# A graph network kernel: six quads of columns made by TensorE in the first layer in place of five, and 40 columns of a chunk gathered in place of 44

## What is computed

```python
W_rel = jnp.matmul(w_comp, V).reshape(num_rels, in_dim, out_dim)     # 90 matrices
e = jnp.concatenate([z_src, z_e, z_dst], axis=1) @ Wa.T              # a score of the edge
msg = jnp.einsum('ei,eio->eo', h_src, W_rel[rel_type]) * e           # first layer
h_out = jax.ops.segment_sum(msg, dst, num_segments=n_nodes)
...
A = edge_emb[edge_type].reshape(-1, MSG_DIM, HID_DIM)                # 8 matrices
msg = jnp.einsum('emh,eh->em', A, h_src)                             # second layer
m = jax.ops.segment_sum(msg, edge_dst, num_segments=N_NODES)         # then a GRU cell
```

## Time and profile before

| | us |
|---|---|
| median of 3 runs | 10946.74 |
| lowest and highest | 10932.45, 10950.66 |
| the profiled execution | 10932.0 |
| its span, first to last instruction | 10930.1 |

### The profile page before, as it was taken

The page is one execution under the profiler, slowest core; times in us unless marked ns, Lnnn a source line. Parts: engine busy times, 40 slices in busy tenths (PEclk is TensorE's granted clock), DMA queues, the critical chain, the costliest instruction groups (busy, mean ns, idle before and its releaser), DMA issues.

```text
span 10930.1 us, 139324 instructions
## 1 busy us (share of the span) xinstructions
PE 5779.2 (53%) x53821; PEld 4786.9 (44%) x53821; DVE 4059.6 (37%) x8932; ACT 4413.2 (40%) x5373; POOL 4678.1 (43%) x4885
## 2 busy tenths in 40 slices
PE   2455555555555555555455555555555555555554
PEld 0244444444444444444344445444544544454453
DVE  2353333344444333333433333333333333333333
ACT  2444334344444433434334344334433443443343
POOL 5434444444444444444344433343344334433434
PEclk6677777777777777777667777777777777776775
DMA  5400000010000001000101101101110111011011
GB/s 157 175 17 21 22 22 22 20 22 22 22 22 22 18 22 22 22 20 22 34 20 10 10 8 10 10 8 10 10 10 8 10 10 10 9 10 10 8 10 12
DMA packets 650830, 252.54 MB, mean 23 GB/s; under 512 B 533184, under 2 KB 623673, under 8 KB 649654
## 3 DMA queue, kind: packets, MB, share of 16 engines
q10 hardware_dynamic: 421870, 84.39, 4.5%
q0 software_dynamic: 156128, 44.51, 4.2%
q1 hardware_dynamic: 72296, 115.06, 3.0%
HBM read 78.24 MB, written 164.99 MB: 22 GB/s over the span
## 4 chain that ended last, share of the span: by engine, by line
PE 48%; issue 42%; ACT 4%; another core or an unknown queue 4%; DMA 1%; DVE 1%; ACTq 0%; SPq 0%; POOL 0%; DVEq 0%; POOLq 0%
PE ps_table L688 39%; PE ps_table L698 5%; PE ps_misc L664 3%; ACT hot_key L872 2%; DMA relation_table<-scanned 1%; ACT hot_type L873 0%; ACT scanned L844 0%; PE ps_table L808 0%; ACTq L828 0%; PE ps_misc L763 0%; DVE scanned L1155 0%; PE ps_table L776 0%; ACT hot_key L877 0%; PE ps_hist L763 0%
## 5 line engine op out<-in xcount | busy, mean ns | idle before, releaser
L688 PE MATMUL ps_table<-node_parts,hot_key 128*128 128x192 bf16 (+1 forms) x44928 | 4668.7, 260 | 2775.8 <-issue 2770.1
L688 PEld LDWEIGHTS ps_table<-node_parts,hot_key 128*128 128x128 bf16 x44928 | 4005.6, 102 | 3362.3 <-issue 3284.4
L872 ACT ACTIVATE hot_key<-ps_misc,less_key 128x512 bf16<-128x512 f16 x3744 | 2216.7, 703 | 5980.5 <-remote 4455.5
L516 POOL DMA_INDIRECT rows<-type_table,idx x2184 | 2065.5, 946 | 3093.1 <-DVE scanned L1155 2418.3
L516 POOL DMA_INDIRECT rows<-relation_table,idx x2288 | 2229.8, 975 | 2674.8 <-DVE scanned L1155 1982.2
L1191 DVE TENSOR_TENSOR picked<-ps_table,hot_tile 128x416 f32<-128x416 f32 x936 | 542.3, 579 | 5272.2 <-remote 4725.4
L877 ACT ACTIVATE hot_key<-hot_key,ones 128x3072 bf16<-128x3072 bf16 (+1 forms) x468 | 1513.9, 3235 | 15.3
L664 PE MATMUL ps_misc<-ident_f,match_cols 128*128 128x128 f16 x3848 | 410.4, 230 | 999.1 <-issue 952.1
L1196 DVE TENSOR_REDUCE source<-picked 128x32 f32<-128x416 f32 x936 | 806.6, 862 | 32.1
L664 PEld LDWEIGHTS ps_misc<-ident_f,match_cols 128*128 128x128 f16 x3848 | 277.1, 101 | 1111.8 <-issue 1045.8
L1205 DVE TENSOR_REDUCE rows<-by_in 128x32 f32<-128x512 f32 (+1 forms) x988 | 694.2, 703 | 33.8
(11 more groups left out here) (207 smaller groups left out, 2037.1 us busy)
## 6 DMA issues: line engine op xcount, KB each, us to landing
scanned<-scanned ACTq DMA_DIRECT2D x52, 992.0 KB
relation_table<-scanned SPq DMA_DIRECT2D x50, 765.0 KB
relation_table<-t_buf SPq DMA_DIRECT2D x48, 765.0 KB
rows<-relation_table,idx POOLq DMA_INDIRECT x2288
rows<-type_table,idx POOLq DMA_INDIRECT x2184
scanned<-scanned ACTq DMA_DIRECT2D x52, 496.0 KB, 7.6
he<-in_edge_attr SPq DMA_DIRECT2D x52, 434.0 KB
type_table<-t_buf SPq DMA_DIRECT2D x14, 448.0 KB
```

Source lines behind the costliest of these rows:

```text
L516: pool.indirect_dma_start(out=rows[:, k, :], out_offset=None, in_=table, in_offset=bass.IndirectOffsetOnAxis(ap=index[:, k:k + 1], axis=0) ...
L688: pe.matmul(ps_table[duo][:, 0, t * BLOCK_W:t * BLOCK_W + width], hot_key[:, b, g, edges], node_parts[:, part, g:TILES:BLOCKS, :], start=( ...
L872: act.activation(hot_key[:, b, g, :], match_bank[:, 0, :], ACT.Abs, bias=less_key[:, g:g + 1])
```

## The change

The number of quads becomes a pair, six for the first layer and five for the second. So the first layer makes 2 + 5 x 4 = 22 columns and gathers 40. The buffers that hold keys and picks of a chunk's made columns grow from 20 to 22 columns. The 32 scans of the chunk before, which were shared out as 0, 4, 8, 12 and 8 over five steps, are shared out as 0, 4, 6, 8, 8 and 6 over six. Scan 15 was the fourth of the fourth step's scans and is now the sixth of the fourth step's. All other edits replace the constant by the layer's own number.

```diff
-QUADS = 5
+QUADS = (6, 5)
...
+        self.quads = QUADS[n]
...
-        self.widths = [DUO] * known + [QUAD] * (QUADS - known)
+        self.widths = [DUO] * known + [QUAD] * (self.quads - known)
         self.share = sum(self.widths)
         self.own = CHUNK - self.share
...
     def half(self, parity, q):
 
-        return (parity * (QUADS - self.known) + q - self.known) % 2
+        return (parity * (self.quads - self.known) + q - self.known) % 2
...
+    SHARE = max(quads * QUAD - known * (QUAD - DUO) for quads, known in zip(QUADS, KNOWN))
...
-        hot_tile = sb("hot_tile", [P, 2, QUADS * QUAD, BLOCK_TILES])
+        hot_tile = sb("hot_tile", [P, 2, SHARE, BLOCK_TILES])
...
             def chunk_by_products(lay, m, parity, last):
 
-                for q in range(QUADS):
-                    if lay.known <= q < QUADS - 1:
+                for q in range(lay.quads):
+                    if lay.known <= q < lay.quads - 1:
                         spread_quad(lay, m, parity, q + 1)
-                    if q == QUADS - 1 and not last:
+                    if q == lay.quads - 1 and not last:
                         spread_quad(lay, m + 1, 1 - parity, lay.known)
                     for duo in range(lay.widths[q] // DUO):
-                        if lay.known and (q, duo) == (QUADS - 2, 1) and not last:
+                        if lay.known and (q, duo) == (lay.quads - 2, 1) and not last:
                             spread_quad(lay, m + 1, 1 - parity, 0)
                         products(lay, m, parity, q, duo)
...
-            SCAN_WITH = (range(0), range(4), range(4, 12), range(12, 24), range(24, 2 * D))
+            SCAN_WITH = (range(0), range(4), range(4, 10), range(10, 18), range(18, 26), range(26, 2 * D))
```

More of the change, by code:

```diff
@@ L659, in spread_quad @@
                 pe.wait_ge(keys_set[lay.n], m + 1)
-                wait_past(pe, match_sb[lay.n], m * QUADS + q)
+                wait_past(pe, match_sb[lay.n], m * lay.quads + q)
                 for k in range(int(q < lay.known), 2):
@@ L668, in products @@
             def products(lay, m, parity, q, duo):
-                quad = m * QUADS + q
+                quad = m * lay.quads + q
                 pe.wait_ge(match_set[lay.n], quad + 1)
@@ L679, in products @@
                 if q >= lay.known:
-                    before = (m, q - 1) if q > lay.known else (m - 1, QUADS - 1)
+                    before = (m, q - 1) if q > lay.known else (m - 1, lay.quads - 1)
                     wait_past(pe, products_used[lay.n], lay.done(*before, duo))
@@ L693, in products @@
                     hot = hot_known[:, :]
-                before = (m, q - 1) if q > 0 and duo * DUO < lay.widths[q - 1] else (m - 1, QUADS - 1)
+                before = (m, q - 1) if q > 0 and duo * DUO < lay.widths[q - 1] else (m - 1, lay.quads - 1)
                 wait_past(pe, products_used[lay.n], lay.done(*before, duo))
@@ L865, in one_hot @@
                 else:
-                    before = (m, q - 2) if q - 2 >= lay.known else (m - 1, q - 2 + QUADS - lay.known)
+                    before = (m, q - 2) if q - 2 >= lay.known else (m - 1, q - 2 + lay.quads - lay.known)
                     wait_past(act, products_ps[lay.n], lay.done(*before, 1))
@@ L884, in chunks_out @@
                 ahead = lay.known + 1
-                for q in range(1 - lay.known, QUADS):
+                for q in range(1 - lay.known, lay.quads):
                     one_hot(lay, 0, 0, q)
@@ L893, in pair @@
                         if not (last and h == 1):
-                            for q in range(ahead, QUADS):
+                            for q in range(ahead, lay.quads):
                                 one_hot(lay, m, 1 - h, q)
@@ L1217, in chunk_rows @@
             def chunk_rows(lay, m, parity, last, between=lambda q: None):
-                steps = m * ((QUADS - lay.known) * ROW_STEPS + 1) + 1
-                for q in range(QUADS):
+                steps = m * ((lay.quads - lay.known) * ROW_STEPS + 1) + 1
+                for q in range(lay.quads):
                     base = steps + (q - lay.known) * ROW_STEPS
-                    if q == QUADS - 3 and not last:
+                    if q == lay.quads - 3 and not last:
                         keys(lay, m + 1, 1 - parity, base)
-                    if q >= QUADS - 3 and not last:
+                    if q >= lay.quads - 3 and not last:
                         base = base + 1
-                    if q + 1 < QUADS or not last:
-                        rest_one_hot(lay, m * QUADS + (q + 1), lay.half(parity, q + 1))
+                    if q + 1 < lay.quads or not last:
+                        rest_one_hot(lay, m * lay.quads + (q + 1), lay.half(parity, q + 1))
                     make_rows(lay, m, parity, q, base, between)
@@ L1284, in pair @@
                     if last and h == 1:
-                        for q in range(QUADS):
+                        for q in range(layers[0].quads):
                             with_quad(q)
@@ L1487, in pair @@
                     if last and h == 1:
-                        for q in range(QUADS):
+                        for q in range(layers[1].quads):
                             with_quad(q)
```

8 lines of the change are left out of this document (4 added, 4 removed).

## The result

| | before | after |
|---|---|---|
| median, us | 10948.7 | 11352.41 |
| lowest and highest | 10932.45, 10951.68 | 11346.32, 11362.29 |
| span of the profiled execution | 10930.1 | 11347.2 |

The changed kernel is slower by 404 us, ratio 1.0373 (95% interval 1.0355 to 1.0391). The forecast was 11290 us, within 11190 to 11430.

A forecast was written before the change was run, and what follows sets the result against it. Gathering and TensorE's work were taken to add. 50 chunks x (9.92 - 5.6 + 0.7) = 251, plus 84 for turns, plus 9, gave +344 us, so 11276, and 11290 us by the runs' median; range 11190 to 11430.

The forecast's parts named there:

- engines independent: Rival: the stop has another cause and 40 gathers end it no sooner; +635 us, 11580 us; chance 3%.
- the stop: Stretch of slowed TensorE during a chunk's gathers, 62.6 us for 44 in the first layer, about 1.4 us per gather.
- The added quad: First layer: one more full quad costs 9.92 us a chunk, as none of it can hide in the stop.
- four gathers: First layer: four gathers fewer shorten the stop by 4 x 1.4 = 5.6 us a chunk.
- The stop's edge: Stop may begin sooner (up to 3.6 us a chunk, +130 us); first gather may shorten (-48 us); neither was taken.
- The loop's turn: First layer: PE's turn after the last quad leaves the stop; 3.5 us for each of 24 turns, 84 us.
- the turn stays hidden: Rival: the first-layer loop's turn still costs nothing; 11206 us, chance 10%.
- What lies in the stop: First layer: the known pair leaves the stop and cheap matmuls take its place; +0.7 us a chunk, from 0 to 0.9.
- The quad in the stop: Rival: the added quad's matmuls fit into the stop, so the kernel gets faster; 10656 us, chance 4%.
- PE starves in it: Rival: ACT cannot make the known pair's one-hot in the stop, PE waits; +95 us, 11385 us; chance 20%.
- The early stop: Stop beginning 5.7 us after the first gather, not 9.3; up to 3.6 us a chunk; 11420 us with starving PE.
- The signs named beforehand: First layer: gathers every 99 us, 102 to 104 every second; full pace after 56 to 57 us; second layer unchanged.

The follow-up runs named there:

- e11: Changed kernel with gathers released one step later and TensorE's first-layer loop written out four times: 11211.09 us, ratio 1.0266 to the kernel before.
- e12: Kernel before with four quads in both layers (48 and 46 gathers), run where the stop exists: 10559.01 us, ratio 0.9507.
- e6: Kernel before, unedited, run in a place without the stop: 6339.41 us.
- e5: Changed kernel, unedited, run in a place without the stop: 6190.98 us, ratio 0.9758 to the kernel before.
- e4: Kernel before with four quads in both layers (48 and 46 gathers), run without the stop: 6901.2 us, ratio 1.0875.

## Why the prediction was right

**The bound.** For the place of its trace the reading holds: gathering and PE's work add. Seven burst lengths lie on one line, 40 gathers for 56.2 us, 42 for 59.0, 44 for 62.6, 46 for 64.8, 48 for 67.6, 84 for 117.8 and 96 for 135.5 (1.40 to 1.42 each). Opposite changes of the number of quads moved the time in opposite directions, +3.7% and -4.9%. But "engines independent", the rival to which I gave 3%, is how the same kernel behaves in another place: there PE passes its duos at full pace amid the gathers and all follows from POOL's beat. The prediction rested on a property of the place and had no row that could tell it from one of the kernel. That the first result came from a place with the stop was luck, for the sign too: of the seven places of this case three have it, and in one of the other four this very change won 2.4%. The Trainium skill's page "Trainium Architecture — The Big Picture", section "Inside one NeuronCore", says that the engines run in parallel and synchronize only through semaphores. For TensorE beside POOL's gathers that agrees with the runs at 6346 us and not with those at 10949 us.

**The added quad, 9.92 us, and four gathers, -5.6.** Right in sum: +4.75 a chunk in e11 against +4.3. There is no run with one of the two alone under the stop.

**The stop's edge, two unknowns left at nothing.** Both occurred. The first gather fell from 1.91 to 0.94 us, and full pace came back after 56.2 us where e11 with its slow first gather has 57.0: -0.8. The stop began 6.9 us after the first gather in place of 8.4: +1.5 to +1.7. My bounds were +3.6 and -0.96. In sum +0.7 to +0.9 a chunk: the period without a turn grew by 100.1 - 94.2 = 5.9 us where I had 5.0, 46 us over 50 chunks. This is the larger of the two terms that were mis-sized; I took neither unknown, as if they cancelled, though one bound was nearly four times the other.

**The loop's turn, 3.5 us.** The chunks with it are 4.4 us longer than those without. Such pairs differ by 0.6 us before and 0.9 in e11 in any case, so the turn itself is worth 3.6 to 3.9. The gap itself is 2.6 us, the low end of what I read in the second layer. The rest goes with the clock: the nine chunks whose clock stays up behind the gap take 102.9 us, 2.7 over those without a turn, which is the gap alone; the 14 in which it drops take 105.6, 2.8 more. At 2213.93 the six matmuls take 1.54 us and the way to the second next transposes 12.2 us (to 2226.15), where from 2419.46 they take 0.87 and 10.7. The second layer's two gaps of the earlier trace rows were the right rows to take it from. That the turn stays hidden (10%) is refuted by the row at 2213.93, and e11 shows what would have kept it hidden.

**What lies in the stop, +0.7.** The known pair's six matmuls are outside of it (2213.93, 1.54 us at a lower clock or 0.87), as predicted. The 0.7 itself does not follow from my rows: 0.86 - 6 x 0.09 is 0.3. And the stop passed 34 or 35 matmuls, not 40 "whatever they are". The pair's cost can't be told from that of the edge; together they are 5.9 - 4.3 = 1.6 us.

**The sum.** 344 us by forecast, 417 between the spans: 73 too few. Two chunks were to grow by 2 x 5.02 + 3.5 = 13.5 us and grew by 204.7 - 188.4 = 16.3; 25 pairs make 70 us. 46 are the edge of the stop, as above. The other 0.9 us a pair, 23 us, lie in the chunks with the turn: I had 3.5 us for it, and gap and clock make 4.4 (2.7, and 2.8 in 14 of 23). I had left out that the clock can drop behind the gap.

**The other rivals.** The quad in the stop: 30 to 38 matmuls pass in it, fewer than before, so no. PE starves in it, because ACT can't make the known pair's one-hot: ACT makes it within the stop, at 2162.73.

```profile
2162.73 0.47 ACT L875 ACTIVATE hot_known<-ps_misc,less_type 90x256 bf16<-90x256 f16 x1 [11.61 <-remote]
```

The early stop that went with that rival did come, at less than half its upper price of 3.6 us; my 11420 us for the two together allowed only 35 us for it, against the 130 of the paragraph before. The signs named beforehand were right in full pace (56.2), in the beat of 99 and 102 to 104 (100 and 105), in one gap of 2.6 us in every second chunk and in the second layer. The waits of ACT over 1 us at full pace, named as a sign against me, are there: 6.51 us behind the turn, and 1.2 to 2.9 us in the chunks without one, in which PE has no gap.

```profile
2318.14 4.73 ACT L874 ACTIVATE hot_key<-ps_misc,less_key 128x512 bf16<-128x512 f16 x8 [2.92 <-PE ps_misc L666]
```

ACT waits there for PE, which has no gap before it, so this wait by itself costs nothing, and as a sign it was badly chosen.

**Open.** What the stop is. It exists in four traces (before, after, e11, e12) and is missing in ten, with unchanged instructions, so it belongs to the chip or its state; no chip whose number is on record was seen in both ways, and that of the first place is not on record. In it PE's results reach DVE and ACT late and PE's issue is slow; whether both have one cause was not tried, since no kernel of mine could bring it about.

## What to carry to other kernels

Before work is moved from one engine to another, find out whether the two engines' times add or overlap, and do so in more than one place: here the chain of the kernel before was 42% "issue" with the stop and 24% without it, and that share was the hint that the first trace gave. Here the best of the three numbers of quads tried with the stop (four, -4.9%) is the worst without it (+8.7%), so a choice that has to hold in both places can't be tuned in one. And where a stretch exists in which an engine can't work anyway, look at which instructions fall into it: moving one wait by a quad brought a turn of 2.6 us of idle time out of it, and moving it back took it in again.

## What the runs showed of the hardware

- The same kernel takes 10949, 10920 or 11107 us in three places and 6339 to 6347 in others. Nothing in its instruction counts or busy times of DVE and ACT differs.
- With the stop a burst of indirect DMAs holds TensorE back for 1.41 us each, 0.16 more than POOL's own beat of 1.25, from 40 to 96 of them. So it outlasts the last gather's issue by more the longer the burst is: by 7.4 us behind 40 (2190.28 to 2197.64), by 15.4 behind the 96 with which e12 begins.
- An indirect DMA costs POOL 0.94 us and 1.25 from start to start, whether it fetches 128 rows or 64 (0.90, 1.205), and mostly 1.9 us, at most 2.5, for one in twenty that falls beside DVE's work (232 of 4472 in e6).
- A turn of PE's loop with six quads costs 2.5 to 3.1 us of idle time where nothing covers it (after, e5), with five 1.9 to 2.6 in the first layer and 3.6 to 4.4 in the second (e6). The page's queue of instruction fetches, per kernel: 511 packets before, 585 after, 537 unrolled, and for four quads this.

```profile
q8 instruction: 40, 0.66, 0.0%
```

So the loops with four quads fetch nothing again when they turn, and those with five do: (511 - 40) packets for 24 turns in the first layer and about as many in the second are ten a turn. The packets' times in the trace say the same: 10 between one turn and the next with five quads in the first layer, 11 or more with six, none with four, and in the first layer one starts 0.9 to 1.6 us behind the branch of every turn. e4, with no packet at its turns, has no gap behind them either. That the gap is the wait for these packets fits all of this.

The Trainium skill's page "Runtime: NRT & Kernel Launch", section "Instruction fetch mechanics", gives TensorE room for 2048 instructions, refilled in blocks of 16 KiB, and says that a taken branch waits for a fetch when its target is not in the current window of two pages. The trace agrees on the blocks: 0.66 MB in 40 packets is 16.5 KB each. It does not agree on two pages of 256 instructions: with four quads a turn goes back over 2 x 356 matmuls and as many weight loads, 1424 instructions (1728 in the second layer), and nothing is fetched. The room of 2048 fits that. As an estimate by that page of the Trainium skill, five quads with 2160 instructions in the second layer and six with 2352 don't fit in it; five in the first layer are 1888 without waits and semaphores and are fetched again all the same, so where the limit lies was not found.
